# Scores of a retention layer on two 64-row halves of the TensorE array, both tiles of a unit in one step, with new engine orders

## What is computed

```python
mod = silu(c) @ wmod                       # sa, ca, ga, sb, cb, gb for each sequence
h = layernorm(x) * (1 + ca) + sa
x = x + ga * retention(h)
h = layernorm(x) * (1 + cb) + sb
x = x + gb * (fwht(silu(h @ W1.T) * (h @ W3.T)) @ W2.T)

# retention: 4 heads, 32 wide in q and k, 64 wide in v
q, k = rope(h @ Wq.T) / sqrt(32), rope(h @ Wk.T)
attn = (q @ k.T) * causal * gamma[h] ** (i - j)
o = attn @ v                               # in chunks, with a state that is carried
o = o * rsqrt(mean(o * o) + eps) * gnorm * silu(h @ Wg.T)
return o @ Wo.T
```

## Time and profile before

| | us |
|---|---|
| median of 3 runs | 277.26 (276.52 to 277.75) |
| profiled execution | 275.44 |
| its span, first to last instruction | 273.5 |
| PE busy in it | 252.9 (92%) |
| PE weight loads busy | 238.5 (87%) |
| DVE, POOL, ACT busy | 172.6, 136.6, 121.5 |
| mean granted clock of TensorE | 0.996 |

### The profile page before, as it was taken

One profiled execution on the slowest core, in us unless ns is written; L12 is line 12 of the kernel. 1 busy time (PEld: TensorE's weight loads), 2 busy tenths in 40 slices (PEclk: granted clock), 3 DMA queues, 4 the chain that ended last, 5 costly groups with the idle time before them and its releaser, 6 DMA issues.

```text
span 273.5 us, 4983 instructions
## 1 busy us (share of the span) xinstructions
PE 252.9 (92%) x1888; PEld 238.5 (87%) x1888; DVE 172.6 (63%) x340; ACT 121.5 (44%) x249; POOL 136.6 (50%) x159
## 2 busy tenths in 40 slices
PE   1698897699999999999999999999999999999992
PEld 1566776599999898999999999999999999999992
DVE  3358897997766684667767756568648556562211
ACT  2427728564373335532642536534453356134320
POOL 3285182359334793254736373744347925434334
PEclk9999999999999999999999999999999999999998
DMA  6998401000100001000100010001100060000102
GB/s 208 351 384 316 153 4 38 1 2 0 42 0 2 0 2 40 0 2 1 41 0 2 0 38 2 0 4 37 41 2 0 2 192 2 0 0 2 41 0 77
DMA packets 11294, 13.89 MB, mean 51 GB/s; under 512 B 1156, under 2 KB 9348, under 8 KB 11016
## 3 DMA queue, kind: packets, MB, share of 16 engines
q1 hardware_dynamic: 11272, 13.58, 15.2%
HBM read 9.64 MB, written 2.11 MB: 43 GB/s over the span
## 4 chain that ended last, share of the span: by engine, by line
PE 78%; POOL 10%; DVE 4%; issue 3%; ACT 2%; DMA 2%; POOLq 0%; SPq 0%; ACTq 0%; DVEq 0%
PE pu L304 31%; PE pacc L304 13%; PE pd L304 7%; PE pa L304 6%; PE pb L304 4%; PE pc L311 3%; PE pc L304 3%; PE pstate L329 2%; POOL rso L793 2%; DMA wmod_sb<-wmod 2%; POOL yo L825 1%; POOL hid_lo L833 1%; PE pa L311 1%; PE pstate L304 1%; POOL rs L793 1%
## 5 line engine op out<-in xcount | busy, mean ns | idle before, releaser
L304 PE MATMUL pu<-h_hi,w_hi 128*128 128x256 f32 x256 | 73.1, 286 | 0.0
L304 PE MATMUL pu<-h_hi,w_lo 128*128 128x256 f32 x256 | 72.5, 283 | 0.0
L304 PE MATMUL pu<-h_lo,w_hi 128*128 128x256 f32 x256 | 72.5, 283 | 0.0
L833 POOL TENSOR_TENSOR hid_lo<-hid,hid_hi 128x512 fp32r<-128x512 f32 x32 | 41.3, 1296 | 49.8 <-ACT hid_hi L781 49.8
L304 PEld LDWEIGHTS pu<-h_hi,w_hi 128*128 128x128 f32 x256 | 49.1, 192 | 0.7 <-DVE h_lo L485 0.3
L304 PEld LDWEIGHTS pu<-h_lo,w_hi 128*128 128x128 f32 x256 | 49.1, 192 | 0.3
L304 PEld LDWEIGHTS pu<-h_hi,w_lo 128*128 128x128 f32 x256 | 49.1, 192 | 0.0
L304 PE MATMUL pacc<-w_hi,hid_hi 128*128 128x256 f32 x128 | 37.3, 291 | 0.7 <-POOL hid_lo L833 0.7
L304 PE MATMUL pacc<-w_lo,hid_hi 128*128 128x256 f32 x128 | 36.2, 283 | 0.0
L304 PE MATMUL pacc<-w_hi,hid_lo 128*128 128x256 f32 x128 | 36.2, 283 | 0.0
L776 ACT ACTIVATE silu<-pu 128x512 f32<-128x512 f32 x32 | 19.0, 594 | 31.5 <-PE pu L304 31.4
(11 more groups left out here) (136 smaller groups left out, 625.2 us busy)
## 6 DMA issues: line engine op xcount, KB each, us to landing
raw<-w SPq DMA_DIRECT2D x4, 512.0 KB, 9.9
out<-xres SPq DMA_DIRECT2D x8, 256.0 KB, 2.4
qb<-qkt SPq DMA_DIRECT2D x28, 64.0 KB, 2.0
xres<-x SPq DMA_DIRECT2D x1, 1536.0 KB, 13.4
raw_w<-w SPq DMA_DIRECT2D x1, 1024.0 KB, 7.9
wmod_sb<-wmod SPq DMA_DIRECT2D x1, 1024.0 KB, 9.8
gates<-gate_dram SPq DMA_DIRECT2D x1, 1024.0 KB
xres<-x SPq DMA_DIRECT2D x2, 256.0 KB, 4.3
```

The lines of the kernel that those rows point to most:

```text
L304: mm = pe.matmul(ps, a, c, start=start and n == 0, stop=stop and n == len(ops) - 1, skip_group_check=True)
L833: pool.tensor_tensor(hid_lo[:, k % 2], hid32[:, k % 2], hid_hi[:, k % 2].bitcast(F32), ALU.subtract).then_inc(p_hid.sem, 1)
```

## The change

`sc` becomes one step for both tiles. The 128 rows are taken as two halves of 64 rows (heads 0 and 1, heads 2 and 3). `qb` shrinks from four to two blocks of columns: within a half, two heads, with the other head's 32 rows zero. For each tile and each of the three products there are two matmuls of 256 columns, one on either half, one behind the other, so 12 a unit instead of 6. The half decides the bank: `pc` holds heads 0 and 1 of both tiles, `pd` heads 2 and 3. The DVE instruction that applies the mask reads both banks. `sc` waits for `pc` and `pd` together, and each `o` waits until both tiles have been read (`d_p` of tile 1). All five orders are new. The diff, cut:

```diff
     "SP": steps(
-        "0:rows 1:qb 2:qb 3:qb 4:qb 5:qb 6:qb 0:out 7:qb 1:out 2:out 3:out 4:out 5:out 6:out 7:out"),
+        "0:rows 1:qb 2:qb 0:out 3:qb 1:out 4:qb 5:qb 6:qb 7:qb 2:out 3:out 4:out 5:out 6:out 7:out"),
     "PE": steps(
-        "0:cols 0:ht 0:qk 0:vg 0:rows 0:cols.1 0:qkt 0:vg.1 0:sc 0:sc.1 1:ht 0:st 0:had 0:had.1 1:qk 0:o 0:st.1 "
-        "0:had.2 0:o.1 1:vg 0:had.3 1:qkt 0:had.4 0:had.5 0:yt 0:proj 1:st 1:vg.1 0:had.6 0:had.7 0:h2t 1:sc "
-        "1:sc.1 0:up 2:ht 1:o 1:o.1 2:qk 2:vg 0:up.1 2:vg.1 1:yt 0:down 2:qkt 1:proj 0:up.2 0:up.3 3:ht 1:h2t "
...
-        "7:qk 5:up.1 6:yt 5:up.2 6:proj 7:st 7:qkt 7:vg.1 5:down 5:down.1 6:h2t 5:up.3 7:sc 7:sc.1 6:up 7:o 7:o.1 "
...
+        "0:cols 0:ht 0:qk 0:vg 0:cols.1 0:qkt 0:vg.1 0:rows 0:st 1:ht 0:st.1 0:sc 1:qk 1:vg 0:o 0:had 0:o.1 "
+        "0:had.1 0:had.2 1:qkt 0:yt 0:had.3 0:proj 0:had.4 1:vg.1 0:had.5 0:had.6 0:h2t 2:ht 0:had.7 1:sc 1:st "
+        "0:up 1:o 2:vg 1:o.1 2:qk 2:vg.1 0:up.1 1:yt 0:down 2:qkt 1:proj 0:up.2 0:up.3 2:st 1:h2t 0:down.1 2:sc "
+        "3:ht 1:up 2:o 2:st.1 0:down.2 2:o.1 3:vg 0:down.3 1:up.1 2:yt 3:qk 3:vg.1 2:proj 1:down 3:qkt 4:ht "
+        "1:up.2 2:h2t 1:up.3 4:qk 3:sc 4:vg 1:down.1 3:st 1:down.2 3:o 4:qkt 3:o.1 2:up 1:down.3 2:up.1 3:yt 4:st "
+        "2:up.2 3:proj 4:vg.1 2:down 2:up.3 3:h2t 5:ht 2:down.1 4:sc 3:up 4:o 2:down.2 4:o.1 5:vg 5:qk 4:st.1 "
...
+        "5:down 7:st 5:down.1 6:h2t 5:up.3 7:sc 6:up 7:o 7:o.1 5:down.2 5:down.3 6:up.1 7:yt 6:down 7:proj 6:up.2 "
+        "6:up.3 7:h2t 6:down.1 6:down.2 7:up 7:up.1 6:down.3 7:up.2 7:down 7:up.3 7:down.1 7:down.2 7:down.3"),
     "DVE": steps(
-        "0:stats 0:norm 0:cols 0:wqk 1:stats 0:hlo 0:rope 1:norm 0:vlo 0:rows 0:qklo 0:cols.1 0:qb 0:vlo.1 0:w2r "
...
+        "0:stats 0:norm 0:cols 0:wqk 1:stats 0:hlo 0:rope 1:norm 0:vlo 0:w2r 0:cols.1 0:qklo 0:qb 0:vlo.1 0:st "
+        "0:rows 1:hlo 0:sc 0:sc.1 0:w2r.1 0:plo 1:rope 0:plo.1 0:o 2:stats 0:ss 0:o.1 3:stats 0:ss.1 0:y 1:vlo "
+        "1:qklo 0:y.1 0:wo 0:w2 0:ytlo 0:st.1 0:w13 0:proj 2:norm 0:norm2 1:vlo.1 0:w13.1 0:w2.1 0:h2lo 0:w2.2 "
...
-        qkt, qb = sb("qkt", [P, E_BUFS, 2, 2, 2, P], F32R), sb("qb", [P, 2, 2, HEADS, P], F32R)
+        qkt, qb = sb("qkt", [P, E_BUFS, 2, 2, 2, P], F32R), sb("qb", [P, 2, 2, 2, P], F32R)
...
-        pa, pb, pc, pd, pstate = (bank(n) for n in "pa pb pc pd pstate".split())
+        pa, pb, pstate = (bank(n) for n in "pa pb pstate".split())
+        pheads = ctx.enter_context(nc.psum_tensor("pheads", [P, 2, 512], F32))
+        pc, pd = pheads[:, 0], pheads[:, 1]
...
-                        sp.dma_start(qb[rows, :, :, h, :].rearrange("p e t i -> p (e t) i").bitcast(F32),
+                        sp.dma_start(qb[rows, :, :, h % 2, :].rearrange("p e t i -> p (e t) i").bitcast(F32),
...
-                    three(pz[k][:, :], [((qkt[:, buf, 0, k, 1], qkt[:, buf, 1, k, 1]),
-                                         (qb[:, 0, k], qb[:, 1, k]))]).then_inc(t_s.sem, 1)
+                    for j in range(2):
+                        for n, (a, c) in enumerate(((0, 0), (0, 1), (1, 0))):
+                            for g in range(2):
+                                rows = slice(g * 2 * DK, (g + 1) * 2 * DK)
+                                mm = pe.matmul(pz[g][:, j * 2 * P:(j + 1) * 2 * P], qkt[rows, buf, a, j, 1],
+                                               qb[rows, c, j].rearrange("p h i -> p (h i)"), start=(n == 0),
+                                               stop=(n == 2), skip_group_check=True)
+                    mm.then_inc(t_s.sem, 1)
...
+                    pe.wait_ge(d_p.sem, d_p.after(u, 1))
                     if t:
-                        pe.wait_ge(d_p.sem, d_p.after(u, k))
...
-                    dve.tensor_tensor(p32[:, k], pz[k][:, :].rearrange("p (h i) -> p h i", h=HEADS),
-                                      causal.unsqueeze(1).to_broadcast([P, HEADS, P]), ALU.mult
+                    dve.wait_ge(t_s.sem, t_s.after(u))
+                    dve.tensor_tensor(p32[:, k].rearrange("p (g h) i -> p g h i", g=2),
+                                      pheads[:, :, k * 2 * P:(k + 1) * 2 * P].rearrange("p g (h i) -> p g h i", h=2),
+                                      causal.unsqueeze(1).unsqueeze(1).to_broadcast([P, 2, 2, P]), ALU.mult
```

More of the change, by code:

```diff
@@ L215, in adaln_block_kernel @@
             sem(n) for n in "t_qk d_rope p_rope t_qkt a_qkt d_qklo a_k p_k".split())
-        t_vg, a_vg, d_vlo, t_s, d_p, a_p, d_plo, t_o, a_o, d_o, a_sq, p_y0, d_ss, p_vo, p_rso, d_y = (
-            sem(n, 2) for n in "t_vg a_vg d_vlo t_s d_p a_p d_plo t_o a_o d_o a_sq p_y0 d_ss p_vo p_rso d_y".split())
-        t_kv, d_s, a_s, p_s = (sem(n) for n in "t_kv d_s a_s p_s".split())
+        t_vg, a_vg, d_vlo, d_p, a_p, d_plo, t_o, a_o, d_o, a_sq, p_y0, d_ss, p_vo, p_rso, d_y = (
+            sem(n, 2) for n in "t_vg a_vg d_vlo d_p a_p d_plo t_o a_o d_o a_sq p_y0 d_ss p_vo p_rso d_y".split())
+        t_s, t_kv, d_s, a_s, p_s = (sem(n) for n in "t_s t_kv d_s a_s p_s".split())
         t_yt, a_yt, d_yt, t_wo, d_br, d_x1, d_st2, d_mv2, p_ve2, p_rs2, d_xn2 = (
@@ L277, in step @@
                         return
-                    sp.wait_ge(t_s.sem, t_s.after(u - 1, 1))
+                    sp.wait_ge(t_s.sem, t_s.after(u - 1))
                     sp.wait_ge(d_qklo.sem, d_qklo.after(u))
@@ L392, in step @@
                     mm.then_inc(t_qkt.sem, 1)
-                elif kind == "sc":
-                    if u == 0 and k == 0:
+                elif kind == "sc" and k == 0:
+                    if u == 0:
                         pe.wait_ge(a_qb0.sem, 1)
                         pe.wait_ge(d_qb0.sem, 1)
-                    elif k == 0:
+                    else:
                         pe.wait_ge(s_qb.sem, s_qb.per * u)
-                    if u and k == 0:
                         pe.wait_ge(a_h2x.sem, a_h2x.after(u - 1))
-                    elif u:
                         pe.wait_ge(d_br.sem, d_br.after(u - 1))
-                    three(pz[k][:, :], [((qkt[:, buf, 0, k, 1], qkt[:, buf, 1, k, 1]),
-                                         (qb[:, 0, k], qb[:, 1, k]))]).then_inc(t_s.sem, 1)
+                    for j in range(2):
[6 more added lines that the diff above has]
+                    mm.then_inc(t_s.sem, 1)
                 elif kind == "st" and t < TILES - 1:
@@ L572, in step @@
                         rows = slice(h * DK, (h + 1) * DK)
-                        ins = dve.tensor_copy(qb[rows, 1, :, h, :], qkt[rows, buf, 1, :, 0].bitcast(F32))
+                        ins = dve.tensor_copy(qb[rows, 1, :, h % 2, :], qkt[rows, buf, 1, :, 0].bitcast(F32))
                     ins.then_inc(d_qb0.sem, 1)
@@ L577, in step @@
                         dve.wait_ge(in_cst.sem, 16)
-                    dve.wait_ge(t_s.sem, t_s.after(u, k))
-                    dve.tensor_tensor(p32[:, k], pz[k][:, :].rearrange("p (h i) -> p h i", h=HEADS),
-                                      causal.unsqueeze(1).to_broadcast([P, HEADS, P]), ALU.mult
+                    dve.wait_ge(t_s.sem, t_s.after(u))
+                    dve.tensor_tensor(p32[:, k].rearrange("p (g h) i -> p g h i", g=2),
+                                      pheads[:, :, k * 2 * P:(k + 1) * 2 * P].rearrange("p g (h i) -> p g h i", h=2),
+                                      causal.unsqueeze(1).unsqueeze(1).to_broadcast([P, 2, 2, P]), ALU.mult
                                       ).then_inc(d_p.sem, 1)
@@ L723, in step @@
                         rows = slice(h * DK, (h + 1) * DK)
-                        ins = act.activation(qb[rows, 0, :, h, :], qkt[rows, buf, 0, :, 0].bitcast(F32),
+                        ins = act.activation(qb[rows, 0, :, h % 2, :], qkt[rows, buf, 0, :, 0].bitcast(F32),
                                              ACT.Copy)
```

## The result

The changed kernel takes 272.04 us (median of 4 runs, 271.05 to 272.66) against 276.89 us for the kernel before on the same chip (4 runs, 275.83 to 277.75): ratio 0.983, 95% interval 0.980 to 0.986. Forecast were 273.2 us and 0.985. The sign, the mechanism (halves side by side) and the size held, but two terms of the sum were too hopeful by 0.7 to 0.8 us each, and a third, the new waits, was too pessimistic by 1.4.

The account below looks back on a forecast made before the run. PE's own work bounds the kernel from the first `up` (52.23 us), a chain through all engines before it. First stretch plus score steps minus new waits, 11.0 - 7c - e = 4.1 us, gives 273.2 us from median 277.26; range 270.5 to 279.0.

Parts of the forecast that it names:

- halves side by side: Score step on PE: both matmuls of a pair run together, 0.72 us a unit before shape changes; 273.2 us, chance 0.58.
- new waits: PE's waits made by the new lists after the first stretch: 0.5 us of loss taken, from 0 to 1.5.
- First stretch: Up to the first `up`: the new orders start it earlier and do `2:ht` before it, gain 2.66 - c.
- The walk: First stretch: new lists followed forward with the durations of before, first `up` at 51 us, good to 1 us.
- Score step, units 2 to 7: On PE in the full stretch: each unit's step falls from 1.39 us to c, gain 6 x (1.39 - c).
- change of shape: Score step: switching between full and half height, twice a unit, 0.10 us each, 0.20 taken from 0 to 0.38.
- c: PE's cost of the new score step per unit: 0.92 us, from 0.72 to 1.10.
- B: Score step: weight loads of both halves queue for one path, 1.56 us a unit; 277.7 us, no change; chance 0.24.
- The pace of 0.113 us: Sixteen full-weight matmuls of only 4 columns take 0.113 us each, suggesting loading 128 columns of weights has its own pace.
- C: Score step: half-row loads are no longer hidden behind the stream before, 2.96 us a unit; 287.5 us, chance 0.08.
- D: New lists: a wait, likeliest a `qb` copy behind an `out` on SP, costs PE 2 to 4 us; 276.2 us, chance 0.10.

Follow-up runs that it names:

- The exchange: Changed kernel with POOL's second part of the w2r split (`0:w2r.1`) moved ahead of the k split of unit 0 (`0:kspl`): 271.92 us, ratio 0.979.
- the experiment: Changed kernel with a full-height matmul of 64 columns between the two tiles' score matmuls: 275.14 us; control with it ahead of the step: 271.93 us.
- two experiments: New score step in the old orders of the kernel before: 278.41 us; changed kernel with POOL's `0:w2r.1` ahead of `0:kspl`: 271.92 us.

## Why the prediction was right, and where it wasn't

Against the profiled execution the sum was 4.06 us; measured were 3.29. Term by term, from PE's timelines of both kernels step by step:

- **First stretch: 1.74 forecast, 0.96 measured.** The first `up` began at 52.32, of which 0.70 us are the first load's later landing (PE waited 6.6 us for it, 5.9 before; in the runs here this wait is 5.9 to 7.2 whatever the kernel). That they pass on whole is taken, not shown: in two more profiles of the changed kernel, with waits of 6.3 and 6.4 us, the first `up` began at 52.64, behind a fall of the clock, and at 52.42. Without that 51.62 against 52.23, 0.61 earlier, and `2:ht` ahead of it brings 0.35. The walk that I held good to 1 us was off by 0.8. The step that failed is the walk with the durations of before: the new orders bring two operations of POOL beside DVE's casts, which took 3.35 us instead of 1.17. The exchange showed it: with the casts at 1.84, `1:qk` came 0.95 us earlier.
- **Score step, units 2 to 7: 2.82 forecast, 2.14 measured.** Side by side was right. The term that was mis-sized is the change of shape: 0.19 (0.20 in the experiment) instead of 0.10. It makes c 1.10 us, the upper end of the range that I gave. The step gains 0.28 us a unit by the run with the old step in the new orders; 0.36 from before to after, because the old step also had small gaps around it in some units.
- **New waits: 0.5 of loss forecast, 0.90 of gain left over.** The 0.90 is what remains of the 3.29 when the other terms are taken off. I costed the new lists only for waits that they add. They also remove some, above all 0.58 us for DVE's `xn` ahead of an `h2t` at 103.9 us (its row stands below); the changed kernel shows no such wait after its first `up`. I put the rest down to gaps of up to 0.4 us around single steps; no run takes them one by one. Neither `out` ahead of `qb` on SP cost anything: PE waits for no `qb` copy.
- **The load's landing: 0.70 of loss**, in no term, and no part of the change.

The wait of 0.58 us in the kernel before:

```profile
103.91 0.65 PE L311 MATMUL pc<-ident,xn 128*128 128x128 f32 x4 [0.58 <-DVE xn L631]
```

So 4.06 - 0.78 - 0.68 + 1.40 - 0.70 = 3.30, which comes out because the third term is the remainder. The total held because errors of opposite sign met, which is luck, within the range that their bounds gave.

The rivals: B (loads in a queue) fell; 12 loads of 0.184 us lie within 0.77 us. The pace of 0.113 us that spoke for it fits loads into the same rows: the six of one half are (0.77 - 0.18) / 5 = 0.12 us apart. The Trainium skill's TensorEngine Tiling (Array Packing), Key Properties, has different tiles loading and multiplying in parallel: this trace agrees, with pairs every 0.12 us; the drain that it names at a change of mode would be the 0.19 to 0.20 us here. C (unhidden loads) fell with the same rows. D's place, a `qb` copy behind an `out`, shows no wait; its mechanism, a wait in the lists that eats the step's gain, is real: with the old lists it came at unit 6, 1.3 us, at a mask instead of a copy.

What I didn't have among the rivals is the one that hid the result of two experiments: a gap on PE in the first stretch can cost twice, once as idle time and again in the clock behind it.

## What to carry to other kernels

Price packing on row halves as pairs plus two changes of shape, 0.12 us a pair and 0.19 to 0.20 a change here, so that it pays only where several pairs stand together and alternate; and rewrite the order with it, since what one merged step finishes later can eat the gain. Where a walk through a new order moves one engine's operation beside another's, read both durations again. And where time saved ahead of a gap doesn't arrive at the end, look at the granted clock behind the gap before looking for a new wait.

## What the runs showed of the hardware

- DVE's casts of 32 partitions took 0.27 to 0.29 us alone and up to 1.26 us beside POOL's two-input operations on 128x512, which took 1.31 us beside them and 1.28 in the kernel before, without them.
- The two halves keep their own place: the first matmul of one started three places ahead of its turn in the list, not six.
- A change between 128 and 64 rows cost 0.19 us in the score step and 0.20 in the experiment with two changes more.
- The granted clock is part of the spread: on one chip the kernel before ran 17 times, 276.1 to 276.8 us with a mean clock of 0.999 to 1.000 (eight runs), and 279.4 to 280.0 with 0.984 (four).
